# Table loads of ScalarE in three stages: a background block one unit later, a background block inside another, and gates by tanh

## What is computed

```python
# conditioning, before every stage (r = x)
num = nf + nb - ekv + euk * vf
den = df + db - ek + euk                      # sums of two scans over time
base = sigmoid(r) * (num / maximum(den, 1e-8))
# layer 1, feed-forward: a mixture of experts with low-rank additions, gates by silu
# layer 2, attention: grouped; q and k are normed per head and rotated (RoPE), softmax,
#   and the mixed values are gated by a sigmoid of a projection
# layer 3, attention: selective state space, E = 512 channels, N = 16 states
h = exp(d[..., None] * A) * h + (d * u)[..., None] * b[:, None, :]   # scan over 256 tokens
y = einsum('ben,bn->be', h, c)
y = (y + u * W_D) * silu(skip)
return y @ W_out.T
```

## Time and profile before

| | us |
|---|---|
| median of 3 runs | 1825.1 (1823.29 to 1829.73) |
| the profiled execution | 1830.95 |
| its span in the trace | 1829.7 |
| busy: TensorE / VectorE / ScalarE / GpSimd | 1564.4 / 1237.5 / 883.1 / 335.0 |

### The profile page before, as it was taken

How to read it: one execution, slowest core, us unless ns; L and a number is a source line. 1 busy time by engine, 2 the same in 40 slices (tenths; PEclk the granted TensorE clock), 3 DMA queues, 4 the chain that set the end, 5 groups by cost and what they waited for, 6 DMA issues and landing times. The chain is left out here.

```text
span 1829.7 us, 16477 instructions
## 1 busy us (share of the span) xinstructions
PE 1564.4 (85%) x5242; PEld 851.2 (47%) x5242; DVE 1237.5 (68%) x2023; ACT 883.1 (48%) x1575; POOL 335.0 (18%) x208
## 2 busy tenths in 40 slices
PE   5998787788898998987999999766768777899998
PEld 2565354357643443443545454323223322357776
DVE  7685466343336626668887888577789899756565
ACT  5454234344323203237887878535656533324453
POOL 1001331331001101100000000000048657313332
PEclk8998999986789999999999999875979989899999
DMA  2002764260030000022111121101000000101110
GB/s 78 1 1 92 261 214 137 72 115 1 1 139 0 0 14 1 1 71 66 33 49 46 49 47 35 68 19 56 20 0 1 1 0 1 39 20 56 52 50 23
DMA packets 45850, 88.21 MB, mean 48 GB/s; under 512 B 10082, under 2 KB 27444, under 8 KB 43462
## 3 DMA queue, kind: packets, MB, share of 16 engines
q1 hardware_dynamic: 40678, 61.48, 11.6%
q0 software_dynamic: 5088, 25.69, 4.1%
HBM read 70.49 MB, written 7.22 MB: 42 GB/s over the span
## 5 line engine op out<-in xcount | busy, mean ns | idle before, releaser
L2895 POOL TENSOR_TENSOR s_bu<-s_rep,s_du 128x1024 f32<-128x1024 f32 x64 | 150.7, 2355 | 636.6 <-ACT s_rep L2812 551.8
L2749 DVE TENSOR_TENSOR_SCAN s_bu<-bank,s_bu 128x1024 f32<-128x1024 f32 x64 | 146.1, 2282 | 14.1 <-ACT bank L2821 14.0
L2984 PE MATMUL bank<-s_bu,ident 128*128 128x512 f32 x256 | 131.6, 640 | 0.9
L159 PE MATMUL bank<-e_xs,e_wsp 128*128 128x512 f32 x528 | 127.8, 391 | 0.7 <-issue 0.7
L2821 ACT ACTIVATE bank<-s_dl,s_an 128x510 f32<-128x510 f32 x128 | 82.8, 682 | 76.4 <-DVE s_bu L2749 76.3
L159 PEld LDWEIGHTS bank<-e_xs,e_wsp 128*128 128x128 f32 x528 | 99.0, 188 | 22.8 <-issue 1.9
L159 PE MATMUL bank<-r_am,r_b 128*128 128x512 f32 x240 | 106.0, 592 | 1.4 <-DVE r_am L1712 1.4
L159 PE MATMUL bank<-conditioned,g_wqk 128*128 128x512 f32 x160 | 79.0, 619 | 5.4 <-ACT g_th L2206 5.1
L1770 ACT ACTIVATE r_sl<-bank 128x512 f32<-128x512 f32 x28 | 16.7, 597 | 136.3 <-PE bank L159 133.2
L2765 DVE TENSOR_TENSOR s_bu<-s_bu,bank 128x1024 f32<-128x1024 f32 x64 | 76.7, 1198 | 7.4 <-PE bank L2915 7.4
L1783 POOL TENSOR_TENSOR r_ys<-r_y,r_y 128x512 f32<-128x512 f32 x14 | 22.9, 1632 | 320.6 <-DVE r_y L1724 320.6
(11 more groups left out here) (505 smaller groups left out, 3620.3 us busy)
## 6 DMA issues: line engine op xcount, KB each, us to landing
g_turn<-g_q SPq DMA_DIRECT2D x64, 128.0 KB, 2.3
e_wgu<-in_e_gu SPq DMA_DIRECT2D x22, 256.0 KB, 2.7
b_vw<-b_values SPq DMA_DIRECT2D x48, 64.0 KB, 3.4
e_wd<-in_e_down SPq DMA_DIRECT2D x22, 128.0 KB, 2.6
r_w<-in_r_w SPq DMA_DIRECT2D x3, 896.0 KB, 8.0
g_wqk<-in_g_qk SPq DMA_DIRECT2D x4, 640.0 KB, 4.0
g_wgv<-in_g_gv SPq DMA_DIRECT2D x4, 640.0 KB, 4.0
g_wo<-in_g_wo SPq DMA_DIRECT2D x4, 512.0 KB, 3.6
```

The lines of the kernel that those rows point to most:

```text
L159: last = e.matmul(out, lhs, rhs, start=start and n == 0, stop=stop and n == len(pairs) - 1, skip_group_check=True)
L2749: e.tensor_tensor_scan(b, flat(k.pairs[n % 2][:, :, :]), b, 0.0, ALU.mult, ALU.add).then_inc(k["s_scanned"].up(), 1)
L2895: e.tensor_tensor(m.bu[n % m.NBU][:, :, :], m.rep[:, 2 * np:2 * np + 2, :], m.du[:, et, half(h)].unsqueeze(1).to_broadcast([P, 2, HALF]), ...
L2984: summed = e.matmul(banks[6][:, :], k.ident[:, :], m.bu[(n - 1) % m.NBU][:, i, :], start=np == 0 and i == 0, stop=np == m.NP - 1 and i == ...
```

## The change

In three places.

*Mixture:* ScalarE doesn't step its background after the first unit of a half, so all its background stands one unit later. VectorE's stays where it was.

*Grouped attention:* the root block is parted into a logarithm over all five, and an exponential over the first two and one over the other three, with two signals; the background (`parted`) gives up the engine between its logarithm and its exponential. In odd turns, where a job ends, the job's logarithm stands behind the roots' logarithm, and its exponential behind the roots' two. In turns 0 and 1 the third tanh moves between the two exponentials.

*Selective stage:* silu(x) is made as x/2 + x/2 * tanh(x/2): ScalarE writes tanh(x/2) and x/2 from the bank, GpSimd multiplies and adds in the turns of `GATE` and the ones after. u * W_D is added by TensorE, with a diagonal matrix that ScalarE makes at the start (`s_diag`), so that VectorE has one product per channel tile. The skip projections stand in the turns of `SKIP`, the tanh in those of `OUT`.

```diff
@@ wkv_scalar
         e.activation(db[:, :], db[:, :], ACT.Ln).then_inc(k.a_steps.sem, 1)
-        e.wait_ge(k.a_steps.sem, k.a_tick())
+        logged = k.a_tick()
+        if parted:
+            yield
+        e.wait_ge(k.a_steps.sem, logged)
         e.activation(db[:, :], db[:, :], ACT.Exp, scale=-1.0).then_inc(k["wkv_inverse"].up(), 1)
@@ lora_scalar
-            step(background, 4)
+            if x:
+                step(background, 4)
@@ grouped_finish
-    e.wait_ge(*k["g_root"].at(f + 1))
+    e.wait_ge(*k["g_root"].at(2 * f + (1 if j < 2 else 2)))
@@ grouped_scalar
-                grouped_root(k, e, new, 0, m.R + 1)
+                grouped_log(k, e, new)
+                if n % 2:
+                    step(background, 1)
+                grouped_root(k, e, new, 0, 2)
+                if old is None:
+                    grouped_tanh(k, e, new, 2)
+                grouped_root(k, e, new, 2, m.R + 1)
+                if n % 2:
+                    step(background, 1)
...
-            if s == 7 and new is not None:
+            if s == 7 and new is not None and old is not None:
                 grouped_tanh(k, e, new, 2)
...
-                step(background, 2)
+                step(background, 1 if s == 5 and n % 2 else 2)
@@ Selective
+    SKIP = [4, 6, 8, 10, 17, 19, 21, 23]
+    OUT = [6, 9, 11, 13, 20, 22, 24, 26]
+    GATE = [8, 11, 22, 24, 26, 28, 30, 32]
@@ selective_output
-    e.scalar_tensor_tensor(o, m.u[:, et, half(h)], k.vcol("s_wd", et), k.banks[6][:, :], ALU.mult, ALU.add).then_inc(k["s_outputs"].up(), 1)
+    e.wait_ge(*k["s_skip_gate"].at(n + 1))
+    e.tensor_tensor(m.y[:, et, half(h)], k.banks[6][:, :], m.sk[:, et, half(h)], ALU.mult).then_inc(k["s_outputs"].up(), 1)
@@ selective_scalar
+    for et in range(ET):
+        e.activation(m.diag[:, et, :], k.ident[:, :], ACT.Copy, scale=k.vcol("s_wd", et)).then_inc(k["s_diag"].up(), 1)
...
-            e.copy(m.sk[:, et_, half(h_)], banks[7][:, :]).then_inc(k["s_skip_out"].up(), 1)
-        if n in (18, 26):
-            h_ = (n - 18) // 8
-            e.wait_ge(*k["s_skip_out"].at(4 * h_ + 4))
-            e.activation(m.sk[:, :, half(h_)], m.sk[:, :, half(h_)], ACT.Silu).then_inc(k["s_skip_gate"].up(), 1)
+            if h_:
+                e.wait_ge(*k["s_skip_gate"].at(q - 3))
+            e.activation(m.th[et_][:, :], banks[7][:, :], ACT.Tanh, scale=0.5).then_inc(k["s_tanh"].up(), 1)
+            e.activation(m.sk[:, et_, half(h_)], banks[7][:, :], ACT.Copy, scale=0.5).then_inc(k["s_skip_out"].up(), 1)
@@ selective_pool
+        if first:
+            e.wait_ge(*k["s_tanh"].at(q + 1))
+            e.wait_ge(*k["s_skip_out"].at(q + 1))
+            e.tensor_tensor(th, th, sk, ALU.mult).then_inc(k["s_tanh_skip"].up(), 1)
+        else:
+            e.wait_ge(*k["s_tanh_skip"].at(q + 1))
+            e.tensor_tensor(sk, sk, th, ALU.add).then_inc(k["s_skip_gate"].up(), 1)
...
+        if n in m.GATE:
+            gate_part(m.GATE.index(n), True)
+        if n - 1 in m.GATE:
+            gate_part(m.GATE.index(n - 1), False)
@@ selective_tensor
+            if np == 4:
+                e.wait_ge(*k["s_diag"].at(4))
+                e.matmul(banks[6][:, :], m.diag[:, et, :], m.u[:, et, half(h)], start=False, stop=False, skip_group_check=True)
```

More of the change, by code:

```diff
@@ L2164, in grouped_variance, with grouped_log @@
     e.activation(m.rs[:, j, :], k.banks[2][:, :], ACT.Identity, scale=1.0 / m.D, bias=k.eps_col(1e-6)).then_inc(k["g_variance"].up(), 1)
+def grouped_log(k, e, f):
+    rs = k.grouped.rs[:, :, :]
+    e.wait_ge(*k["g_variance"].at(5 * f + 5))
+    e.activation(rs, rs, ACT.Ln).then_inc(k["g_logged"].up(), 1)
 def grouped_root(k, e, f, first, last):
[L2168 to L2172 removed]
+    rs = k.grouped.rs[:, first:last, :]
+    e.wait_ge(*k["g_logged"].at(f + 1))
     e.activation(rs, rs, ACT.Exp, scale=-0.5).then_inc(k["g_root"].up(), 1)
@@ L2880, in selective_pool, with gate_part @@
     m = k.selective
+    def gate_part(q, first):
+        h, et = divmod(q, 4)
+        th, sk = m.th[et][:, :], m.sk[:, et, half(h)]
+        if first:
[5 more added lines that the diff above has]
+            e.tensor_tensor(sk, sk, th, ALU.add).then_inc(k["s_skip_gate"].up(), 1)
     for n, (h, et, np) in enumerate(m.JOBS):
@@ L2990, in selective_tensor @@
             spread_b(2 * (n - 25) + 17)
-        if 9 <= n < 25:
-            q, c = divmod(n - 9, CT)
+        for q, first in enumerate(m.SKIP):
             h, et = divmod(q, 4)
-            if q == 0:
-                e.wait_ge(*k["s_rep"].at(16))
-            else:
-                e.wait_ge(*k["s_skip_out"].at(q))
-            part = e.matmul(banks[7][:, :], m.wsk[:, c, tile(et)], k.XC[:, c, half(h)], start=c == 0, stop=c == CT - 1, skip_group_check=True)
-            if c == CT - 1:
-                part.then_inc(k["s_skip"].up(), 1)
+            if n == first:
+                e.wait_ge(*(k["s_skip_out"].at(q) if q else k["s_rep"].at(16)))
+            for c in ((0, 1) if n == first and q == 0 else (n - first,) if n - first in (0, 1) and q else ()):
+                part = e.matmul(banks[7][:, :], m.wsk[:, c, tile(et)], k.XC[:, c, half(h)], start=c == 0, stop=c == CT - 1, skip_group_check=True)
+                if c == CT - 1:
+                    part.then_inc(k["s_skip"].up(), 1)
         if 37 <= n < 45:
```

28 lines of the change are left out of this document (6 added, 22 removed).

## The result

The changed kernel takes 1781.9 us (median of 4 runs, 1781.1 to 1782.6) against 1827.4 of the kernel before, measured beside it; the ratio is 0.9753, 95% interval 0.9731 to 0.9775. The forecast was 1782. The profiled execution has a span of 1781.0 us, 48.7 less than before. TensorE is busy 1550.0 us, ScalarE 868.8 (14 fewer), GpSimd 351.6.

A forecast was written before the change was run, and what follows sets the result against it. TensorE was taken to bound the mixture and grouped attention, VectorE the selective stage, each waiting for ScalarE. Gains of 14.6 + 15.8 + 12.6 = 43.0 us off the 1825.1 median gave 1782.1, say 1782; range 1769 to 1801.

The forecast's parts named there:

- Mixture, 14.6: Mixture, both halves: TensorE's waits shrink or go and its clock holds; 6.2 + 4.6 + 2.2 + 1.6 = 14.6 us gained.
- clock term of 4.6: Mixture: without the waits of 3.10 us, the eight matmuls behind them run at full clock, 2.9 and 1.7 us gained.
- Grouped attention, 15.8: Grouped attention: TensorE waits less for ScalarE's root block in turns 0, 1, 3, 5, 7, with clock; 15.8 us gained.
- 2.6 less, 0.6 back: Grouped attention, turn 1: wait for the copy behind the block 2.6 less, 0.6 back for the third tanh; 2.0 us gained.
- Selective stage, 12.6: Selective stage: gains 8.8 + 8.0 = 16.8 us, losses 1.2 + 0.9 + 2.1 = 4.2; net 12.6 us gained.
- the four waits: Selective stage: VectorE's waits of 2.44 and 2.46 for decays, 1.08 and 2.05 for spreads; 8.0 us gained.
- 2.1 + 0.9: Selective stage losses: 2.1 us for GpSimd's slower pace and TensorE's spreads, 0.9 for the diagonal product in turn 29.
- the start: Selective stage: four small 128x128 activations ahead of the spreads, 0.3 us each, 1.2 us lost.
- no wait over 1 us: Selective stage sign: no wait of VectorE over 1 us between turns 9 and 30.
- 3.55 from 23 to 33: Selective stage sign: pace about 3.55 us a turn from turn 23 to 33, GpSimd without idle there.
- rival 1: Mixture and grouped attention: stalls move on, half of 14.6 + 15.8 is lost, 1797 us; chance 0.13.
- Rival 5: Table loads: each takes its own length once more from the pipeline, 15.4 us more gained, 1767 us; chance 0.04.

The follow-up runs named there:

- e8: The changed kernel with GpSimd's gate products of the second half eight turns later (turns 34 to 41 in place of 26 to 33); 1785.2 us, single execution.
- e5_split: The changed kernel with the job's logarithm and exponential back ahead of the roots, with their own two loads; the parting stays; 1796.9 us, single execution.
- e1: The kernel before with the mixture's lag alone; median 1814.8 us against 1829.0, ratio 0.9934.
- e2: The kernel before with the change of grouped attention alone; median 1812.9 us against 1829.0, ratio 0.9913.

## Why the prediction was right, and where it was not

The median came within 0.2 us of the forecast; that closeness is luck. The forecast was a saving of 43.0 us off the median of three runs, 1825.1; measured were 45.5 off a median of four, 1827.4, and 48.7 between the two profiles. Taken off 1827.4, the same 43.0 would have given 1784.4. By stage the means over all profiles with the old and with the changed code of a stage are the better measure: 13.6 us in the mixture (three with the old code, eight with the new; forecast 14.6), 16.7 in grouped attention (three and five; 15.8), 13.8 in the scans (three and seven; 12.6).

One slip of the text: the chances of the cases that the range takes in add up to about 0.9, not to the 8 in 10 it gives.

*Mixture, 14.6.* The waits are right to the tenth: 3.10 and 0.83 gone, 1.59 down to 0.54, in both halves. The clock term of 4.6 was measured as 4.3 in the pair of profiles, but it belongs to that execution: the old code behind these two waits lost 2.9 + 1.7, 1.6 + 0 and 1.7 + 1.5 us in three executions, 3.1 in the mean. This term is mis-sized for that reason. That the same stage loses up to 3.4 us without a wait was in no term.

*Grouped attention, 15.8.* Seen are 16.2 to 17.0 in the table. Turn 0: 1.3, as forecast, and 0.8 of clock that was not counted. Turn 3: 5.4 in the pair, 6.4 against the others; turn 5: 5.4 and 3.7 (forecast 5.1 and 5.0). Turn 7: 2.8 (2.4). Behind turn 7 the pair shows 2.8 more, which no term had and which is no work of the change: with nearly the same waits (0.6 to 1.4 us each) the changed code takes 91.4 to 98.4 us from turn 7's projections to the end of the stage. **The step that failed is turn 1's "2.6 less, 0.6 back"**: it let ScalarE's chain move up as a whole by the loads that go, but ScalarE then stood 1.57 and 1.12 us before its tanhs for banks that TensorE had not filled, and two functions of 1.04 us now stand in the block ahead of the copy. From the logarithm's load to the copy it is 10.35 us (843.12 to 853.47) where it was 7.88 (862.30 to 870.18). Before, with TensorE's first wait, then the changed kernel:

```profile
861.94 3.67 PE L159 MATMUL bank<-conditioned,g_wgv 128*128 128x512 f32 x8 [1.02 <-ACT g_th L2206]
862.30 1.28 ACT L2171 ACT_TABLE_LOAD   x1
870.18 0.56 ACT L2198 COPY g_pt<-bank 128x512 f32<-128x512 f32 x1
```

```profile
843.12 1.28 ACT L2176 ACT_TABLE_LOAD   x1
853.47 0.57 ACT L2208 COPY g_pt<-bank 128x512 f32<-128x512 f32 x1
```

In place of the 2.0 that were to go, TensorE's waits in the turn grew by 0.9 us, and the turn's length gave 0.1 (one execution, e8, has 1.0: 47.6 us). e5_split shows that the two loads are worth nothing there: the job stands outside again and the turn is as long. The sum hid it, since turns 0, 3, 5 and 7 and the end of the stage gave more than forecast in the pair.

*Selective stage, 12.6.* Seen are 15.1 in the pair; in three executions the old code took 247.9 to 251.8 us, the new 235.7 to 236.9. Right: the four waits (8.0 forecast; turns 19, 27, 28 and 29 gave 8.7, of which 0.6 is turn 29's gate product) and the gate products (8.8 forecast; turns 42, 50 and 58 gave 1.5 each, turn 35 1.9, turns 29, 31 and 33 0.6 each, and the eighth lies behind the last scan). GpSimd's products, the diagonal products and the spreads, forecast at 2.1 + 0.9, took back 2.6 in turns 24, 25 and 28 to 34. Mis-sized: the start was 0.5 to 0.7 and not 1.2; ScalarE's four small activations take 1.26 us together, and its next wait for TensorE falls from 0.70 to 0.48. Missed: 1.2 lost at scan 11, where the tanh of turn 9 waits 3.06 us for its projection and so holds the decays and the logarithm behind it. The 2.2 won at turns 44 and 45 was not forecast either, and is clock: in the pair they take 8.8 and 6.6 us, but 7.7 in e1 and e2 with the old code and 6.6 or 7.7 with the new, as shown above. Whether the shorter wait makes the good case likelier is not shown. The forecast sign "no wait over 1 us" was thus wrong at one place, and "3.55 from 23 to 33" held at five of eleven turns only (25, 29, 30, 31 and 33).

*The rivals.* Stalls moved on in turn 1 alone, 1.9 us of the 15 that rival 1 wanted. Behind the waits that went the clock came back. GpSimd's products cost 2.6 us at most, together with the spreads, and not 18. Rival 5's second price of a load is excluded: two loads put back in e5_split bring waits of 3.59 and 3.52 us in the turns where VectorE's 1.0 us comes on top, and 2.64 where it doesn't, close to 2 x 1.28. The Trainium skill (ScalarE: Activation LUTs, What ACT_TABLE_LOAD costs) would have had 2.66 us for each; by the rows it is 1.28.
